# Sending the inverse softmax sums through DRAM instead of through TensorE transposes

## What is computed

```python
scores = jnp.einsum('bqhd,bkhd->bhqk', q_full, k_full) * scale
scores = jnp.where(causal[None, None], scores, -1e30)
probs = jax.nn.softmax(scores, axis=-1)
attn = jnp.einsum('bhqk,bkhd->bqhd', probs, v)
attn.reshape(b, s, NH * DV) @ w_o
```

## Time and profile before

| | |
|---|---|
| Time, median of 3 runs | 1439.94 us (1437.68 to 1440.76) |
| The profiled execution, its own time | 1432.93 us |
| Its span | 1430.9 us |
| PE busy | 1208.2 us (84%), 7492 matmuls |
| PE weight loads busy | 966.0 us (68%) |
| DVE busy | 841.9 us (59%) |
| ACT busy | 672.2 us (47%) |
| POOL busy | 312.9 us (22%) |
| Mean granted TensorE clock | 0.92 of full |
| DMA | 41.85 MB, mean 29 GB/s |

### The profile page before, as it was taken

One profiled execution on the slowest core, in us unless ns is written; L12 is line 12 of the kernel. 1 busy time (PEld: TensorE's weight loads), 2 busy tenths in 40 slices (PEclk: granted clock), 3 DMA queues, 4 the chain that ended last, 5 costly groups with the idle time before them and its releaser, 6 DMA issues.

```text
span 1430.9 us, 25754 instructions
## 1 busy us (share of the span) xinstructions
PE 1208.2 (84%) x7492; PEld 966.0 (68%) x7492; DVE 841.9 (59%) x2575; ACT 672.2 (47%) x1922; POOL 312.9 (22%) x366
## 2 busy tenths in 40 slices
PE   6799996999789995999599995999599987984573
PEld 4588765886678774876588675876488676862341
DVE  3377664766667674767467674767477565742121
ACT  1377533762457443752466344753366345730120
POOL 1000034002400133002500232002500241014574
PEclk7899997999989997999899997999799997997786
DMA  9000001000100010000100020000100010004463
GB/s 293 26 0 0 1 16 44 0 0 15 44 0 0 0 57 2 0 0 15 44 0 0 0 59 0 0 0 15 44 0 0 15 29 0 0 1 136 110 152 51
DMA packets 44852, 41.85 MB, mean 29 GB/s; under 512 B 10800, under 2 KB 41496, under 8 KB 44832
## 3 DMA queue, kind: packets, MB, share of 16 engines
q1 hardware_dynamic: 24864, 26.58, 6.2%
q0 software_dynamic: 7936, 6.38, 2.7%
q10 hardware_dynamic: 12032, 8.65, 2.1%
HBM read 30.84 MB, written 10.81 MB: 29 GB/s over the span
## 4 chain that ended last, share of the span: by engine, by line
PE 66%; DVE 9%; issue 9%; another core or an unknown queue 5%; POOL 4%; DMA 3%; ACT 2%; DVEq 0%; POOLq 0%; SPq 0%; ACTq 0%
PE PS L672 9%; PE PS L693 8%; PE PS L651 6%; PE PS L652 5%; PE PS L653 5%; PE PS L783 5%; PE PS L637 4%; PE PS L813 3%; PE PS L791 3%; PE PS L774 2%; PE PS L776 2%; PE PS L624 2%; PE PS L627 2%; PE PS L625 2%
## 5 line engine op out<-in xcount | busy, mean ns | idle before, releaser
L959 ACT ACTIVATE probs<-probs,nmax 128x512 f32<-128x512 f32 (+3 forms) x512 | 283.7, 555 | 183.0 <-DVE nmax L1215 179.3
L1215 DVE CUSTOM_DVE_ANT_0 probs<-PS,cmask 128x512 f32<-128x512 f32 (+3 forms) x512 | 231.5, 489 | 129.9 <-PE PS L653 126.9
L651 PE MATMUL PS<-kTh,qTh 128*128 128x512 f32 (+3 forms) x512 | 180.4, 352 | 66.7 <-DVE pT L1232 65.1
L672 PE MATMUL PS<-ident,probs 128*128 128x128 f32 x1280 | 169.2, 277 | 30.9 <-ACT pT L968 23.0
L968 ACT ACTIVATE pT<-PS 128x384 f32<-128x384 f32 (+3 forms) x320 | 125.3, 460 | 142.5 <-remote 71.6
L672 PEld LDWEIGHTS PS<-ident,probs 128*128 128x128 f32 x1280 | 142.5, 141 | 43.5 <-ACT pT L968 25.1
L462 POOL TENSOR_SCALAR rstd<-mv 128x4 f32<-128x4 f32 (+2 forms) x24 | 5.6, 232 | 757.5 <-DVE mv L1167 569.7
L652 PE MATMUL PS<-kTl,qTh 128*128 128x512 f32 (+3 forms) x512 | 169.8, 332 | 0.0
L653 PE MATMUL PS<-kTh,qTl 128*128 128x512 f32 (+3 forms) x512 | 169.7, 331 | 0.0
L651 PEld LDWEIGHTS PS<-kTh,qTh 128*128 128x128 f32 x512 | 100.6, 196 | 78.8 <-DVE pT L1232 67.9
L693 PE MATMUL PS<-pT,kmat 128*64 128x512 f32 (+3 forms) x1024 | 152.0, 439 | 0.3 <-issue 0.3
(11 more groups left out here) (216 smaller groups left out, 2194.8 us busy)
## 6 DMA issues: line engine op xcount, KB each, us to landing
x_in<-in_x SPq DMA_DIRECT2D x8, 512.0 KB
modb<-mod_dram SPq DMA_DIRECT2D x8, 512.0 KB
h_dram<-h SPq DMA_DIRECT2D x8, 512.0 KB, 2.9
out<-base SPq DMA_DIRECT2D x8, 512.0 KB, 3.4
pT<-in_wo SPq DMA_DIRECT2D x1, 2048.0 KB, 11.8
tab_dram<-entry,slot POOLq DMA_INDIRECT x128
oT<-in_wqnT SPq DMA_DIRECT2D x1, 1536.0 KB, 10.1
pT<-in_egate ACTq DMA_DIRECT2D x6, 176.0 KB
```

The costliest lines, as they stand in the source:

```text
L651: pe.matmul(PS[:, bank, 0:n], qTh[:, h, rows_q], kTh[:, 0:n], start=True, stop=False)
L672: mm = pe.transpose(PS[:, bank, col:col + P], probs[:, UO[u] + j * P:UO[u] + (j + 1) * P], ident[:])
L959: act.activation(probs[:, UO[u]:UO[u] + UW[u]], probs[:, UO[u]:UO[u] + UW[u]], ACT.Exp, scale=-1.0, bias=nmax[:, u:u + 1], accum_out=psums ...
L1215: dve.tensor_tensor_reduce(out=probs[:, UO[u]:UO[u] + UW[u]], in0=PS[:, SBANK[u], 0:UW[u]], in1=cmask[:, S - UW[u]:S], scale=-1.0, scalar= ...
```

## The change

The inverse sums go another way. DVE still inverts the 8 sums (`prec`), whose columns now stand in the order head, query tile (`UC`). SP writes `prec` to a new DRAM buffer `inv_dram` of 8 x 128 numbers (the 128x8 tile turned by the addressing), waits until that has landed and until the previous pair's `values_out` has read `rb`, and then reads it back in two DMAs, each a head's 512 numbers (2 KB) broadcast to 64 partitions of `rb`. `rb` is a tile of its own now. `values_out` waits for both (`rb_landed`), and `invert_sums` waits until the previous `prec` has been stored. DVE's widening copy, PE's 4 transposes and ACT's copy are gone, with the waits on them. SP takes this once for each pair, between its batch transfers: `store_batch` is split into `store_h2` and `store_base`, and pair 0 of the next batch is served between the two.

```diff
--- before.py
+++ after.py
@@ -41,17 +41,17 @@
 UNITS = [(h, i) for h in range(2) for i in range(NT - 1, -1, -1)]
 NU = len(UNITS)
 UW = [(i + 1) * P for _, i in UNITS]
+UC = [h * NT + i for h, i in UNITS]
 UO = [sum(UW[:u]) for u in range(NU)]
 SBANK = [0, 1, 2, 0, 1, 2, 0, 1]
 
 GROUPS = [((0,), 3), ((1,), 4), ((2, 3), 2), ((4,), 0), ((5,), 1), ((6, 7), 3)]
-RBANK = 4
 OBANK, QBANKS = 5, [6, 7]
 KV_ORDER = [2, 0, 1, 3]
 SA, CA, GA, SB, CB, GB = range(6)
 
 
-CHAIN_PROLOGUE, CHAIN_PAIR, CHAIN_BATCH = 37, 4, 84
+CHAIN_PROLOGUE, CHAIN_PAIR, CHAIN_BATCH = 36, 3, 76
 
 
 COUNT_STEPS = NT + 2
@@ -82,6 +82,7 @@
     mod_dram = nc.dram_tensor("mod_dram", (B, 4 * H), F32, kind="Internal").ap()
     gb_dram = nc.dram_tensor("gb_dram", (B, H), F32, kind="Internal").ap()
     h2_dram = nc.dram_tensor("h2_dram", (T + P, H), F32, kind="Internal").ap()
+    inv_dram = nc.dram_tensor("inv_dram", (NU, P), F32, kind="Internal").ap()
     tab_dram = nc.dram_tensor("tab_dram", (NE * CAP, 2), F32, kind="Internal").ap()
 
     def wait_alone(eng, semaphore, value):
@@ -180,8 +181,7 @@
 
         th = sb("th", [P, S])
         mid = sb("mid", [P, S])
-        wide = mid
-        rb = th
+        rb = sb("rb", [P, S])
         midT = sb("midT", [P, 3, S])
         lgT = sb("lgT", [NE, S])
         lmax = sb("lmax", [P, NT])
@@ -290,9 +290,9 @@
         s_ps = sem("s_ps")
         max_ready = sem("max_ready")
         exp_ready = sem("exp_ready")
-        wide_ready = sem("wide_ready")
-        r_ps = sem("r_ps")
-        rb_ready = sem("rb_ready")
+        prec_ready = sem("prec_ready")
+        inv_out = sem("inv_out")
+        rb_landed = sem("rb_landed")
         pT_ps = sem("pT_ps")
         pT_act = sem("pT_act")
         pT_dve = sem("pT_dve")
@@ -404,21 +404,42 @@
                              mod_dram[bass.ds(b, 1), :].rearrange("a n -> (a n)").partition_broadcast(P)
                              ).then_inc(modb_landed, 16)
 
-            def store_batch(b):
+            def store_h2(b):
                 sp.wait_ge(h2_ready, b + 1)
                 sp.dma_start(rows(h2_dram, b), h2[:]).then_inc(h2_out, 16)
+
+            def store_base(b):
                 sp.wait_ge(base_ready, b + 2)
                 sp.dma_start(rows(outr, b), base[:]).then_inc(base_out, 16)
 
+            def spread_sums(g):
+                sp.wait_ge(prec_ready, g + 1)
+                sp.wait_ge(rb_landed, 32 * g + 32)
+                sp.dma_start(inv_dram.rearrange("u p -> p u"), prec[:], allow_slow_non_contiguous=True).then_inc(inv_out, 16)
+                sp.wait_ge(inv_out, 16 * g + 32)
+                sp.wait_ge(oT_ready, g + 1)
+                for h in range(2):
+                    sp.dma_start(rb[h * KL:(h + 1) * KL, :],
+                                 inv_dram[h * NT:(h + 1) * NT, :].rearrange("t p -> (t p)").partition_broadcast(KL)
+                                 ).then_inc(rb_landed, 16)
+
             load_modb(0)
+            spread_sums(0)
             with sp.Fori(0, B - 1) as b:
                 n = b + 1
                 sp.wait_ge(h1_ready, n)
                 sp.wait_ge(res_ready, n)
                 sp.dma_start(x_in[:], rows(xr, n)).then_inc(x_landed, 16)
-                store_batch(b)
+                with sp.Fori(1, NPAIR) as p:
+                    spread_sums(b * NPAIR + p)
+                store_h2(b)
+                spread_sums(n * NPAIR)
+                store_base(b)
                 load_modb(n)
-            store_batch(B - 1)
+            with sp.Fori(1, NPAIR) as p:
+                spread_sums(LAST * NPAIR + p)
+            store_h2(LAST)
+            store_base(LAST)
 
             sp.wait_ge(scattered, B * NT * TOPK * 16)
             sp.dma_start(tab[:], tab_dram.rearrange("(p e) c -> p e c", p=P)).then_inc(tab_landed, 16)
@@ -662,8 +683,6 @@
                         pe.wait_ge(max_ready, g * NU + k + 4)
                     if k == 0 and not first:
                         pe.wait_ge(pT_dve, 2 * g)
-                    if k == 1 and not first:
-                        pe.wait_ge(rb_ready, g)
                     if k == 5:
                         pe.wait_ge(pT_act, 4 * g + 1)
                     col = 0
@@ -673,14 +692,6 @@
                                               ident[:])
                             col += P
                     mm.then_inc(pT_ps, 1)
-
-            def spread_sums(g):
-
-                pe.wait_ge(wide_ready, g + 1)
-                pe.wait_ge(pT_act, 4 * g + 2)
-                for t in range(NT):
-                    mm = pe.transpose(PS[:, RBANK, bass.ts(t, P)], wide[:, bass.ts(NT - 1 - t, P)], ident[:])
-                mm.then_inc(r_ps, 1)
 
             def values(g, b):
 
@@ -728,7 +739,6 @@
                 if last and more:
                     turn_h1(b + 1, 1)
                 turn_probs(g, first, (4, 5))
-                spread_sums(g)
                 if not last:
                     scores(g + 1, False, (0, 1, 2))
                 if first and more:
@@ -936,6 +946,8 @@
         def _(act):
 
             act.sem_inc(oT_ready, 1)
+            act.sem_inc(inv_out, 16)
+            act.sem_inc(rb_landed, 32)
             act.sem_inc(h2_out, 16)
             act.sem_inc(base_out, 16)
             act.sem_inc(base_ready, 1)
@@ -957,7 +969,7 @@
                 for u in units:
                     act.wait_ge(max_ready, g * NU + u + 1)
                     act.activation(probs[:, UO[u]:UO[u] + UW[u]], probs[:, UO[u]:UO[u] + UW[u]], ACT.Exp, scale=-1.0,
-                                   bias=nmax[:, u:u + 1], accum_out=psums[:, u:u + 1]).then_inc(exp_ready, 1)
+                                   bias=nmax[:, u:u + 1], accum_out=psums[:, UC[u]:UC[u] + 1]).then_inc(exp_ready, 1)
 
             def group_out(g, k):
                 units, bank = GROUPS[k]
@@ -969,11 +981,6 @@
                                         PS[:, bank, col:col + UW[u]].rearrange("p (j q) -> p j q", q=P), ACT.Copy)
                     col += UW[u]
                 cp.then_inc(pT_act, 1)
-
-            def sums_out(g):
-                act.wait_ge(r_ps, g + 1)
-                act.wait_ge(oT_ready, g + 1)
-                act.activation(rb[:], PS[:, RBANK, :], ACT.Copy).then_inc(rb_ready, 1)
 
             def step(p, b, last, more):
                 g = b * NPAIR + p
@@ -990,7 +997,6 @@
                     turned_h1(b + 1)
                 group_out(g, 2)
                 group_out(g, 4)
-                sums_out(g)
                 if not last:
                     exps(g + 1, (0, 1, 2))
 
@@ -1218,10 +1224,8 @@
 
             def invert_sums(g):
                 dve.wait_ge(exp_ready, g * NU + NU)
-                ch.step(dve.reciprocal(prec[:], psums[:]))
-                dve.tensor_copy(wide[:].rearrange("p (t h d) -> p h t d", t=NT, h=2),
-                                prec[:].rearrange("p (h t) -> p h t", h=2).unsqueeze(3).to_broadcast(
-                                    [P, 2, NT, KL])).then_inc(wide_ready, 1)
+                dve.wait_ge(inv_out, 16 * g + 16)
+                dve.reciprocal(prec[:], psums[:]).then_inc(prec_ready, 1)
 
             def group_out(g, k):
                 units, bank = GROUPS[k]
@@ -1237,7 +1241,7 @@
             def values_out(p, g):
 
                 dve.wait_ge(o_ps, g + 1)
-                dve.wait_ge(rb_ready, g + 1)
+                dve.wait_ge(rb_landed, 32 * g + 64)
                 dve.tensor_tensor(oT[:, p, :], PS[:, OBANK, :], rb[:], ALU.mult).then_inc(oT_ready, 1)
 
             def q_low(g, h):
```

## The result

The changed kernel takes 1598.95 us (median of 4 runs, 1594.86 to 1604.44), the kernel before 1438.91 (4 runs, 1437.68 to 1440.76): 1.112 times as long, 95% interval 1.109 to 1.116. The profiled execution took 1595.38 us, its span is 1593.4. The forecast was 1439.9 us with a range of 1412 to 1462. The case that came is rival 2: the transfer sets the period.

What follows compares the result with a forecast made beforehand. The prediction took a tie between PE's thread and the ACT-DVE thread to set the next scores. Removal 0 and additions 0 left 1432.93 us for the profiled execution, 1439.9 us on the median, range 1412 to 1462.

Steps and rivals of the forecast that it cites:

- rival 2: At DVE's wait for `rb_landed`: slow single-element store, transfer sets the period beyond 12.2 us; 1570 us at 14 us, chance 0.09.
- The removal is worth nothing: Dropping PE's four transposes, ACT's copy and DVE's widening copy in each pair was put at 0 us.
- The tie: Before the next pair's scores, PE arrives at 426.59 and the ACT-DVE thread lets it go on at 426.68, 0.09 us later.
- the chain's 0.44 us: Time the profile's chain charged to PE's four transposes in each pair; 28.2 us if all lay on the path.
- Rival 1: PE's transposes were on the path: 0.44 us in 49 pairs, 21.6 us faster, 1418 us; chance 0.16.
- The store takes 3.3 us: SP's store of `prec`: 64 packets per DMA engine at 24 ns, 1.5 us, plus 1.8 us for the bare round.
- The broadcasts take 2.7 us and 0.4 us for the second issue: SP's two reads into `rb`, 256 KB in 128 packets of 2 KB: between 1.8 and 4.8 us, 2.7 taken.
- The time available is 12.6 us, and 10.4 in `middle`: From `prec` ready to `values_out`; a 6.7 us transfer would land 5.9 us early, in `middle` 3.7 us early.
- The price in rival 2: Each us beyond 12.2 costs a us in some 56 pairs, 2 us more in `middle`; 130 us at 14 us.
- Rival 3: DMAs disturb other engines: 192 us slower (1632), or the scatter's stretch 23 us longer (1462); chance 0.09 together.
- the smaller form of the rival: DMAs lengthen only POOL's scatter stretch by 3.3 us, 7 times: 23 us, 1462 us; two thirds of the 0.09.
- PE's clock: Loss of PE's clock from idling 0.53 us in a pair, put at 0.

Runs made afterwards that it cites:

- without any exchange: Changed kernel with the three DMAs of each pair left out and `rb` filled with ones once: 1423.52 us, 0.997 of the kernel before.
- The experiment with the numbers apart: Changed kernel with the 1024 numbers stored 64 bytes apart in a second DRAM buffer, broadcasts reading a constant: 1434.91 us, 1.004 of the kernel before.
- two buffers: Changed kernel with two DRAM buffers in turn, the store no longer waiting for the previous broadcasts: 1537.64 us, 1.078 of the kernel before.
- pieces of 32 bytes: Changed kernel storing each partition's 8 numbers side by side, 128 pieces, so sums reach wrong queries: 1432.98 us, 1.004 of the kernel before.
- the single executions at 32 and at 256 bytes: Changed kernel with the numbers stored 32 or 256 bytes apart, one execution each: 1306.65 and 1306.82 us, against 1307.82 before.
- the reordered before: Kernel before with PE's transposes and ACT's copies in a new order, its old exchange kept: 1312.77 us, 1.003 of the kernel before.

## Why the prediction was wrong

- *The removal is worth nothing.* Right. The tie read from the timeline holds, against the chain's 0.44 us: period 12.19 without the old way. "The reader is to see 0.5 us of idle in PE's load and 1.1 us in `q_low`": 0.50 and 1.14. Rival 1 is out: without any exchange the median is 0.3% lower and the period is the same.
- *The store takes 3.3 us.* This term failed. It measured 10.4 us in the median (7.8 to 12.2), three times as much, and always above its upper bound of 6.6. Both prices for a packet, 24 and 57 ns, came from packets that touch nothing in common, and I multiplied one of them by 64, as though packets only queued in their engine. The experiment with the numbers apart shows that this sum was fair for such packets, even high: 2.6 us. No row that the prediction uses shows 4-byte writes to neighbouring addresses, so the bound from above was no bound. It should have been drawn from the addresses too: 16 numbers of 4 bytes in each 64, from 16 partitions. The fixed 2 us that the prediction quotes for every DMA stand in a section of the Trainium skill on DMAs issued from POOL ("DMA: Bandwidth & Descriptors", "Anatomy of one DMA"); the good stores here, issued from SP, had rounds of 1.2 and 1.4 us.
- *The broadcasts take 2.7 us and 0.4 us for the second issue.* Near: 4.66 us from the first issue to the release of `values_out`, against 3.1 forecast and a bound of 5.2; in the other middle pairs it is 3.4 to 5.3. The two issues last 1.09 us together, where 0.8 was assumed.
- *The time available is 12.6 us, and 10.4 in `middle`.* Right as numbers, and where each transfer is seen alone. But the change's store waits for the previous broadcasts (`rb_landed`). The prediction doesn't name this wait, so it stands there at nothing; with a transfer of 6.7 us it would have cost nothing. With one of over 12.2 us it turns a latency with a whole pair of room into a ring, in which nothing overlaps: the transfer's length is then the period. The point from which rival 2 decides was placed well, but it was reasoned from DVE's wait alone; two buffers give back a third of the loss (7.8% instead of 11.2%).
- *The price in rival 2.* It put 130 us on a transfer of 14 us. With what was measured, 14.6 us for the mean step and 14.8 for `middle`, the same sum gives (14.6 - 12.2) x 56 + (14.8 - 10.0) x 8 = 173 us, against 162.5.
- *The chance.* 0.09 for this case was too small. The reason given was the distance from 24 ns and 57 ns to 109 ns; but a price that no row shows, of a kind (neighbouring 4-byte writes) that no row shows, deserved a range of several times. The Trainium skill ("DMA: Bandwidth & Descriptors", "Rules for kernel authors") warned of one descriptor for each element and of reordering by a plain DMA. Its advice was right here; the count of descriptors as the reason isn't borne out, since 1024 of them took 2.6 us. Nor is the Trainium skill's rule on transfers under 512 bytes (same page, "Specifications") enough by itself: pieces of 32 bytes had a round of 1.4 us.
- *Rival 3, disturbance by DMAs.* Small but there, on the first chip: the kernels with the exchange and a period of 12.19 lie 9.5 and 11.4 us above the one without, with all pairs outside the scatter's stretch alike. In the profiles the steps through `middle` and pair 1 sum to 588.8 us over the seven batches without the exchange, 592.6 with pieces of 32 bytes and 598.6 with the numbers 64 bytes apart; but in the kernel before, which has no such DMAs, they are 601.8. So the smaller form of the rival is possible, not shown. On the other chips, which have no such stretch, the single executions at 32 and at 256 bytes lay 1 us below before.
- *PE's clock.* The forecast set its loss at 0. The mean granted clock fell from 0.92 to 0.893, with PE idle for some us in many pairs; PE carries only 23% of the chain there, and no run tells what this cost.

## What to carry to other kernels

A small tensor that is turned by a DMA's addressing has a price that goes, in these runs, by how many separate 4-byte writes fall into the same 64 bytes or so of DRAM, and little by its bytes or the count of its packets: turn it on an engine first and store whole rows, or keep the numbers apart. When a diff adds a wait between a transfer and the one before it, compare the transfer with the loop's period and not only with the time until its use. And when the chain and a timeline disagree on what a removal brings, follow each thread to the instruction at which they meet, and write down when the third one arrives as well.

## What was not expected of the hardware

- Writes of 4 bytes to neighbouring addresses: about 0.5 us for each further number in a stretch of 64 bytes, 16 of them some 10 us, while the DMA engines show under 1 us of packets. The profile's busy shares can't show this; the waits of the queue that issues the next DMA do.
- The same kernel before took 1427.8 and 1438.9 us in the comparisons on the first chips and 1307.8 to 1308.9 on the later ones. In the profiled execution of before, the step of `values_out` in pair 1 of a batch is 25 to 28 us, under POOL's scatter; in that of the reordered before on a later chip it is 12.2. With the step in front of it, it is 85.7 us against 68.0, and 7 times 17.7 are 124 of the 120 to 130 us. In the slow stretch ACT and DVE stand idle behind PE's transposes, and the profile can't say what ended it (for ACT's copy L968 71.6 us over the run). The later chip's profile of the reordered before has no such idle time. Why the runs differ in this, and whether it is the chip, wasn't found, and it moved no verdict here, since each kernel was compared with before on its own chip.
- On the changed kernel the same stall moved: step of pair 1 15.7 us instead of 25.1, and 72.9 instead of 60.6 in the step before it, with a "remote" wait of up to 19.9 us in `values_out`. The stall seems tied to the stretch and not to one instruction: PE itself, which waits for nothing that the profile shows, issues single transposes there 2 to 3 us apart (from 426.82 to 439.68 us of the span).
